# Perceiver cross-attention: attention values as TensorE's stationary operand, one output bank for a pair of groups

## The reference, cut to what matters

```python
xn, ln_lat = layer_norm(x, g1, b1), layer_norm(latents, g2, b2)   # context, latents; D = 256
q = ln_lat @ Wq                                                   # 16 heads of 64
k, v = split(concatenate([xn, ln_lat], axis=1) @ Wkv)
weight = einsum('bhld,bhnd->bhln', q, k) / 8, masked
weight = softmax(weight, axis=-1)
out = einsum('bhln,bhnd->bhld', weight, v) @ Wout
```

## Time and profile before

| | us |
|---|---|
| median of 3 runs (1054.81 to 1055.64) | 1055.42 |
| the profiled execution | 1054.65 |
| its span, first to last instruction | 1052.8 |
| TensorE busy, of the span | 1014.3 |
| VectorE busy | 809.3 |
| ScalarE busy | 666.8 |
| GpSimd busy | 204.1 |

### The profile page before, as it was taken

One profiled execution on the slowest core, in us unless ns is written; L12 is line 12 of the kernel. 1 busy time (PEld: TensorE's weight loads), 2 busy tenths in 40 slices (PEclk: granted clock), 3 DMA queues, 4 the chain that ended last, 5 costly groups with the idle time before them and its releaser, 6 DMA issues. The chain is left out here.

```text
span 1052.8 us, 25657 instructions
## 1 busy us (share of the span) xinstructions
PE 1014.3 (96%) x8683; PEld 943.1 (90%) x8684; DVE 809.3 (77%) x3001; ACT 666.8 (63%) x1550; POOL 204.1 (19%) x265
## 2 busy tenths in 40 slices
PE   6999999999999999999999998988999999999997
PEld 6899999999999999999999998977888999889887
DVE  7887777685877786787787777579879889889753
ACT  4765565674665665566565566478776876767753
POOL 0111111110111111111111111342015203263213
PEclk9999999999999999999999999999999999999999
DMA  6000000000000000000000100520010000110000
GB/s 208 18 13 2 10 1 1 12 12 4 12 2 0 12 13 3 13 2 0 12 13 2 35 2 2 166 38 2 1 41 21 2 1 21 35 48 2 1 22 21
DMA packets 28803, 21.64 MB, mean 21 GB/s; under 512 B 12094, under 2 KB 26267, under 8 KB 28699
## 3 DMA queue, kind: packets, MB, share of 16 engines
q1 hardware_dynamic: 28529, 20.21, 6.5%
q10 hardware_dynamic: 170, 0.07, 0.0%
HBM read 19.17 MB, written 1.05 MB: 19 GB/s over the span
## 5 line engine op out<-in xcount | busy, mean ns | idle before, releaser
L303 PEld LDWEIGHTS pv_ps<-v,pt 128*128 128x128 f32 x1792 | 214.9, 192 | 9.3 <-issue 2.8
L303 PE MATMUL pv_ps<-v,pt 128*128 128x65 f32 x1792 | 215.2, 272 | 3.2 <-DVE o L818 1.8
L796 DVE CUSTOM_DVE_ANT_0 s_sb<-s_ps,pen,mstate 128x256 f32<-128x256 f32 (+1 forms) x512 | 199.9, 446 | 13.9 <-issue 11.0
L510 ACT ACTIVATE probs<-s_sb,mbias 128x256 f32<-128x256 f32 (+1 forms) x512 | 203.2, 470 | 0.0
L670 POOL TENSOR_TENSOR o<-o,alpha 128x260 f32<-128x260 f32 x128 | 85.7, 669 | 561.3 <-ACT alpha L504 561.3
L519 ACT ACTIVATE pt<-turn 128x512 f32<-128x512 f32 x128 | 76.2, 595 | 123.0 <-PE turn L290 109.1
L290 PE MATMUL turn<-ident,probs 128*128 128x128 f32 x896 | 123.8, 278 | 0.1
L290 PEld LDWEIGHTS turn<-ident,probs 128*128 128x128 f32 x896 | 98.8, 145 | 9.5 <-issue 0.3
L818 DVE TENSOR_TENSOR o<-o,pv_ps 128x260 f32<-128x260 f32 x128 | 53.9, 421 | 46.1 <-PE pv_ps L303 34.7
L279 PE MATMUL s_ps<-kh,qh 64*128 64x256 f32 (+1 forms) x512 | 78.9, 304 | 2.9 <-DVE x L840 1.6
L768 DVE TENSOR_TENSOR kl<-proj,kh 128x512 fp32r<-128x512 f32 (+1 forms) x63 | 41.3, 655 | 51.5 <-ACT kh L497 51.0
(11 more groups left out here) (432 smaller groups left out, 2730.7 us busy)
## 6 DMA issues: line engine op xcount, KB each, us to landing
raw<-in_ctx SPq DMA_DIRECT2D x24, 128.0 KB, 2.0
f_wqkv_raw<-in_L_ffn_wqkv SPq DMA_DIRECT2D x6, 512.0 KB, 5.3
f_w_raw<-in_L_ffn_w SPq DMA_DIRECT2D x8, 256.0 KB, 5.1
f_w_raw<-in_L_ffn_w SPq DMA_DIRECT2D x2, 640.0 KB
wkv_raw<-in_L_xattn_Wkv SPq DMA_DIRECT2D x1, 1024.0 KB, 8.5
wout_raw<-in_L_xattn_Wout SPq DMA_DIRECT2D x1, 1024.0 KB, 12.5
f_wo_raw<-in_L_ffn_wo SPq DMA_DIRECT2D x2, 512.0 KB, 4.7
x<-in_x SPq DMA_DIRECT2D x1, 768.0 KB, 9.6
```

The lines of the kernel that those rows point to most:

```text
L303: last = pe.matmul(t.pv_ps[:, u, :], t.pt[g % 2][:, u, kt, :], t.v[:, kt, h, :], start=(kt == 0), stop=(kt == kts - 1))
L510: last = act.activation(t.probs[g % 2][:, u, 0:kts * P], t.s_sb[g % 2][:, u, 0:kts * P], ACT.Exp, bias=t.mbias[:, at:at + 1], scale=0.125)
L796: last = dve.tensor_tensor_reduce(out=t.s_sb[g % 2][:, u, 0:width], in0=t.s_ps[g % 2][:, u, 0:width], in1=t.pen[:, 0:width], scale=1.0, sc ...
```

## The change

Values become the stationary operand and the turned probabilities the moving one. A group then takes 4 matmuls (2 in a half body) with 64 stationary columns and 256 moving columns each, in fp32 as before; the first head's output goes to partitions 0 to 63 of `pv_ps`, the second's to 64 to 127. The bank now holds two groups, the even one in its first half and the odd one in its second. Since the output is the wrong way round, ScalarE copies the bank to a new buffer `ov` (`store_outputs`), TensorE turns it back with 4 transposes into the same bank (`turn_back`), and VectorE adds both groups at once (`add_outputs`). The 65th column goes: ScalarE's exponentials also give their sums (`accum_out`), and GpSimd adds these to `o`'s 65th column. TensorE's `weighted_values` of an odd group stands ahead of the projection in an even step, that of an even group behind the projection in an odd step, as before. `turn_back` opens an odd step. VectorE's addition comes in odd steps, behind `maxima`. Two small buffers and two semaphores of the opening are shared with others, to make room.

```diff
@@ -187,6 +187,10 @@
         if j < 0:
             return None if prev is None else (m - 1, j + NG, KINDS[prev])
         return None
+
+    def pair_at(m, kind, prev, j):
+
+        return at_step(m, kind, prev, j - 4) if j % 2 else None
 
     with nc.Block() as block:
         @block.sync
@@ -295,14 +299,21 @@
                 pe.wait_ge(s["pt_ready"], 16 * m + 2 * g + 2)
                 if g % 4 == 0:
                     pe.wait_ge(s["v_ready"], 4 * m + g // 2 + 2)
-                if g or not isinstance(m, int):
+                if g % 2 == 0 and (g or not isinstance(m, int)):
                     pe.wait_ge(s["o_added"], 8 * m + g)
-                for u in range(GU):
-                    h = 2 * g + u // QT
-                    for kt in range(kts):
-                        last = pe.matmul(t.pv_ps[:, u, :], t.pt[g % 2][:, u, kt, :], t.v[:, kt, h, :],
+                for kt in range(kts):
+                    for o, rows in enumerate((slice(0, DH), slice(DH, P))):
+                        last = pe.matmul(t.pv_ps[rows, g % 2, :], t.v[:, kt, 2 * g + o, :], t.pt[g % 2][:, QT * o:QT * o + QT, kt, :],
                                          start=(kt == 0), stop=(kt == kts - 1))
                 last.then_inc(s["pv_done"], 1)
+
+            def turn_back(m, g, kts):
+
+                pe.wait_ge(s["ov_stored"], 8 * m + g + 1)
+                for k in range(2):
+                    for qt in range(QT):
+                        last = pe.transpose(t.pv_ps[:, qt, k * P:(k + 1) * P], t.ov[:, k, qt * P:(qt + 1) * P], t.ident[:])
+                last.then_inc(s["o_turned_back"], 2)
 
             def turn_output(b, u):
 
@@ -384,9 +395,15 @@
                             scores(m, g, KINDS[kind])
                     if prev is None and j == 2:
                         pe.wait_ge(s["q_ready"], 4)
+                    pair = pair_at(m, kind, prev, j)
+                    if pair:
+                        turn_back(*pair)
                     now = at_step(m, kind, prev, j - 2)
                     if now:
                         turn_probs(*now)
+                    now = at_step(m, kind, prev, j - 3)
+                    if now and j % 2 == 0:
+                        weighted_values(*now)
                     if finish and j in (1, 2, 4, 5):
                         u = {1: 0, 2: 1, 4: 2, 5: 3}[j]
                         if u % 2 == 0:
@@ -437,7 +454,7 @@
                     now = at_step(m, kind, prev, j - 3)
                     if prev is None and j == 3:
                         pe.wait_ge(s["plan_rows"], 1)
-                    if now:
+                    if now and j % 2:
                         weighted_values(*now)
                     if kind and j == 3 and not final:
                         pe.wait_ge(s["v_ready"], 4 * m + (3 if KINDS[kind] == 2 else 4))
@@ -508,8 +525,15 @@
                 for u in range(GU):
                     at = GU * g + u
                     last = act.activation(t.probs[g % 2][:, u, 0:kts * P], t.s_sb[g % 2][:, u, 0:kts * P], ACT.Exp,
-                                          bias=t.mbias[:, at:at + 1], scale=0.125)
+                                          bias=t.mbias[:, at:at + 1], scale=0.125, accum_out=t.sums[:, at:at + 1])
                 last.then_inc(s["p_ready"], 1)
+
+            def store_outputs(m, g, kts):
+
+                act.wait_ge(s["pv_done"], 8 * m + g + 1)
+                if g >= 2 or not isinstance(m, int):
+                    act.wait_ge(s["o_turned_back"], 8 * m + g - 1)
+                act.activation(t.ov[:], t.pv_ps[:], ACT.Copy).then_inc(s["ov_stored"], 2)
 
             def store_turned(m, g, kts):
                 act.wait_ge(s["t_done"], 8 * m + g + 1)
@@ -542,6 +566,9 @@
                     now = at_step(m, kind, prev, j - 2)
                     if now:
                         store_turned(*now)
+                    now = at_step(m, kind, prev, j - 3)
+                    if now and j % 2 == 0:
+                        store_outputs(*now)
                     if finish and j in (1, 2, 4, 5):
                         store_output(b, {1: 0, 2: 1, 4: 2, 5: 3}[j], kind)
                     if final and j == 2:
@@ -669,6 +696,9 @@
                         pool.wait_ge(s["o_added"], 8 * m + g - 7)
                     pool.tensor_tensor(t.o[:, cols, :], t.o[:, cols, :],
                                        t.alpha[:, cols].unsqueeze(2).broadcast_to([P, GU, DH + 1]), ALU.mult).then_inc(s["rescaled"], 1)
+                    pool.wait_ge(s["rescaled"], 16 * m + 2 * g + 1)
+                    pool.wait_ge(s["p_ready"], 8 * m + g + 1)
+                    pool.tensor_tensor(t.o[:, cols, DH], t.o[:, cols, DH], t.sums[:, cols], ALU.add).then_inc(s["rescaled"], 1)
 
             pool.memset(t.o[:], 0.0).then_inc(s["state_zero"], 1)
             walk(pool, body)
@@ -811,15 +840,17 @@
                     dve.wait_ge(s["pv_done"], 8 * m + g - 1)
                 dve.tensor_copy(t.pt[g % 2][:, 2:4, :, :].rearrange("p u k q -> p (u k q)"), t.turn[1][:]).then_inc(s["pt_ready"], 1)
 
-            def add_output(m, g, kts):
-                cols = slice(GU * g, GU * (g + 1))
-                dve.wait_ge(s["pv_done"], 8 * m + g + 1)
-                dve.wait_ge(s["rescaled"], 8 * m + g + 1)
-                dve.tensor_tensor(t.o[:, cols, :], t.o[:, cols, :], t.pv_ps[:], ALU.add).then_inc(s["o_added"], 1)
+            def add_outputs(m, g, kts):
+                cols = slice(GU * (g - 1), GU * (g + 1))
+                dve.wait_ge(s["o_turned_back"], 8 * m + g + 1)
+                dve.wait_ge(s["rescaled"], 16 * m + 2 * g + 1)
+                added = t.o[:, cols, 0:DH].rearrange("p (h q) d -> p h q d", q=QT)
+                dve.tensor_tensor(added, added, t.pv_ps[:].rearrange("p q (h d) -> p h q d", d=DH), ALU.add).then_inc(s["o_added"], 2)
 
             def normalise_output(m, b, half):
                 cols = slice(half * H, (half + 1) * H)
                 dve.wait_ge(s["o_added"], 8 * m - 4 + 4 * half)
+                dve.wait_ge(s["rescaled"], 16 * m - 8 + 8 * half)
                 dve.reciprocal(t.inv[:, cols], t.o[:, cols, DH]).then_inc(s["inverse"], 1)
                 dve.wait_ge(s["inverse"], 2 * b - 2 + half + 1)
                 dve.tensor_tensor(t.onorm[:, :, half * 512:(half + 1) * 512].rearrange("p q (h d) -> p h q d", h=NG),
@@ -849,18 +880,20 @@
                 if kind == "latents":
                     dve.wait_ge(s["state_set"], b + 1)
                 for j in range(NG if kind else 6):
-                    now = at_step(m, kind, prev, j - 4)
-                    if now:
-                        add_output(*now)
-                    if finish and j in (0, 3):
-                        normalise_output(m, b, j // 3)
+                    if finish and j == 0:
+                        normalise_output(m, b, 0)
                     if kind and j == 4 and not final:
                         gained(m + 1, which)
                     if kind:
                         maxima(m, j, KINDS[kind])
+                    pair = pair_at(m, kind, prev, j)
+                    if pair:
+                        add_outputs(*pair)
                     now = at_step(m, kind, prev, j - 2)
                     if now:
                         store_turned(*now)
+                    if finish and j == 3:
+                        normalise_output(m, b, 1)
                     if finish and j in (1, 2, 4, 5):
                         output_lo(b, {1: 0, 2: 1, 4: 2, 5: 3}[j], kind)
                     if kind is None and j == 1:
@@ -2560,19 +2593,22 @@
...
-            t.v = sb("v", [P, KT, H, DH + 1])
+            t.v = sb("v", [P, KT, H, DH])
+            t.ov = sb("ov", [P, 2, L])
-            t.pv_ps = ctx.enter_context(nc.psum_tensor("pv_ps", [P, GU, DH + 1], F32))
+            t.pv_ps = ctx.enter_context(nc.psum_tensor("pv_ps", [P, 2, L], F32))
```

More of the change, by code:

```diff
@@ L159, in value_part @@
     def value_part(u):
-        return t.v[:, u % 2, (u // 2) * NG:(u // 2 + 1) * NG, 0:DH]
+        return t.v[:, u % 2, (u // 2) * NG:(u // 2 + 1) * NG, :]
     def load_norm(eng, which):
@@ L465, in _ @@
             project_keys(0, KB)
-            pe.wait_ge(s["keys_spread"], 1)
-            pe.matmul(t.pv_ps[0:B, 1, 0:NCH + 1], t.row_of[:], t.listed[:], start=True, stop=True).then_inc(s["keys_listed"], 1)
+            pe.wait_ge(s["flags_ready"], 3)
+            pe.matmul(t.pv_ps[0:B, 1, 0:NCH + 1], t.row_of[:], t.listed[:], start=True, stop=True).then_inc(s["flags_ranked"], 1)
             pe.wait_ge(s["w_lo"], 3)
@@ L502, in softmax_part @@
                 if not isinstance(m, int):
-                    act.wait_ge(s["rescaled"], 8 * m + g - 7)
+                    act.wait_ge(s["rescaled"], 16 * m + 2 * g - 14)
                 act.activation(t.alpha[:, GU * g:GU * (g + 1)], t.mdiff[:, GU * g:GU * (g + 1)], ACT.Exp,
@@ L679, in _ @@
             dve.memset(t.tick[:], 0.0).then_inc(s["s_read"], 2)
```

(17 more changed lines are left out.)

4 lines of the change are left out of this document (2 added, 2 removed).

## The result

The changed kernel takes 1147.2 us (median of 4 runs, 1143.9 to 1150.9); the kernel before took 1055.1 beside it. The ratio is 1.088, 95% interval 1.084 to 1.091: 92 us slower. 1106 was forecast, from 1074 to 1178.

What follows compares the result with a forecast made beforehand. TensorE bounds the cross stage, but would wait for VectorE's addition: 1054.65 + 27 (pair) + 13.5 (half) + 3.5 (last half) + 2.4 (latents) + 3 (opening) + 1 (drain) = 1105, forecast 1106 us, range 1074 to 1178.

Steps and rivals of the forecast that it cites:

- the rival without any overlap: `weighted_values`: the two heads' matmuls do not overlap, W = 1.87 us, w = 1.01; 1173 us in all; chance 0.22.
- a wait for the addition: TensorE idles some 2.4, 1.5 and 1.5 us before `weighted_values` in steps 1, 5 and 7 of a pair body.
- VectorE's wait for `kh`: Sign in the changed profile: this wait grows from 0.6 to about 1.8 us.
- The chain: Odd-step `weighted_values` waits through projection, `kl`, statistics, maxima and addition; steps 0 and 1 take 11.7 us, now 9.8.
- The price W: Time of `weighted_values` in a full group: 1.22 us, from five slots of 0.215 plus 0.15 for switching tile shape.
- the full-overlap rival: `weighted_values`: the two heads overlap fully, W = 1.01 us, w = 0.58; 1083 us in all; chance 0.12.
- the fifth slot: In-order starts let head 1's high pass run only with head 0's low pass: 8 records take 5 slots, 1.07 us.
- The prediction's last sentence: A granted clock below full after the new idle would add to all of it; no size given.
- the finishing bodies: Latents bodies that finish a batch: +0.8 us each, three times, 2.4 in all.
- the drain: End of the stage: a longer path from the last values to the sum, +1 us.
- VectorE's 1.5 us of lateness in step 1: Finishing latents bodies: statistics make VectorE late by some 1.5 us in step 1, the only step where maxima start late.
- The faster rival: VectorE's addition is in time, so TensorE's own sum holds: 8 x -2.3 us in pair bodies; 1033 us; chance 0.09.

Runs made afterwards that it cites:

- the fillers: Changed kernel plus unread identity transposes on TensorE in step 1 of pair bodies and steps 1 and 5 of half bodies: 1117.25 us, ratio 1.059.
- the last kernel: Kernel with addition ahead of maxima and values and copy late (1044.85 us), early order restored from step 4 of half bodies and in the drain: 1038.81 us.

## Why the prediction was right

*The range, and luck.* 1147.2 us is 41 above the forecast, and outside the forecast's own range (1090 to 1125). It falls in the wide range because that made room up to 1178 for the rival without any overlap, and this rival did not come true. So the mechanism was right, and that the wide range held is luck: a term that was left out, the clock, came to less than the room kept for something else.

*The mechanism.* The forecast was a wait for the addition, behind the maxima of the odd step. The changed profile shows it where the prediction put it (2.34, 1.23 and 1.19 us in steps 1, 5 and 7 of a pair body; 2.4, 1.5 and 1.5 were named), and the kernel with the addition first takes it away and all of the loss with it. VectorE's wait for `kh` grew from 0.61 to 1.81 us, as forecast, and TensorE is busy 87% of the stage.

*The chain.* Each link came out: the projection at 3.65 us (2.45 + 1.22 = 3.67), `kl` 2.36 later (2.34), the statistics' end 1.6 later (1.57), maxima 2.2. Steps 4 and 5 take 10.67 us, 10.8 forecast. Without the clock's loss the pair body is 42.75 us, 43.1 forecast, and the half body 37.35, 37.7 forecast.

*The price W.* 1.22 was forecast, 1.19 measured, by two errors that cancel, which is luck again: four slots, not five (full overlap, which I had given 0.12 as a rival), each of 0.216 as priced; but 0.18 us ahead of the group and some 0.15 at its ends where the forecast had 0.15 in all. So the full-overlap rival (the prediction once calls it the second) fails on its price, 1.01, not on its mechanism. The Trainium skill's rule for the swap ("TensorEngine Tiling (Array Packing)", section Performance Considerations) agrees with the trace, four slots instead of eight; the switch takes back a quarter of it, 0.18 of 1.74 - 1.02. The Trainium skill's statement that matmuls keep program order ("TensorE: Matmul & The Clock Gate", Part 3), from which I drew the fifth slot, did not tell the slots here, in either order of the heads; which two records share a start the trace does not name.

*The step that was mis-sized: the clock.* The prediction's last sentence said that a lower granted clock would add, and put no number to it. It was some 30 of the 41 us between 1106 and 1147. The earlier trace rows could not price it, but the trace they are from could. TensorE waits 1.38 us there at 650.65, in the last steps of the stage, and behind that:

```profile
651.30:654.70 3.40, 3.40 (x19) 3.40 (x18) 1.36 (x3) 1.47 (x3) 0.00 (x0) 0.50 0.00 0
```

Eight forecast idles of 2.4 us and sixteen of 1.5 asked for a term. How large one is for a given wait the runs do not settle: 2.35 us cost some 1.5 in seven pair bodies and nothing in the first, and the half bodies lost 7.4, 4.4 and 1.5 us to the clock (against 37.35 with the fillers) behind the same two waits. What decides between them is open. With that the sum of the parts is: pair bodies +37 (27 forecast), half +26 (13.5), opening +3.6 (3).

*Also too small: the finishing bodies and the drain.* Finishing latents bodies +13.7 (2.4), last half body and drain +10.7 (4.5). Waits in the first of them, in the changed kernel's trace:

```profile
252.84 0.65 PE L306 MATMUL pv_ps<-pt,v 128*64 128x256 f32 x4 [2.24 <-DVE o L848]
264.15 1.08 PE L306 MATMUL pv_ps<-pt,v 128*64 128x256 f32 x8 [0.83 <-DVE o L848]
```

I took VectorE's 1.5 us of lateness in step 1, and none in step 3. Part of it is the clock again (0.72 in the mean from 254 to 260 us). The second such body has the same waits but a full clock, and lasts 51.5 us where the two others last 53.1: so some 3 of the 13.7 us are the clock. With the addition first such a body lasts 48.95 at full clock: some 8 are the addition's place, and the last 3 stay even then. For the drain the shares are not separated.

*Smaller slips.* ScalarE copies the bank 64 times, that is 16 bodies' worth and not 8 (38.3 us busy in the changed kernel); it changes no term of the sum.

*The faster rival* (the addition in time, 1033 us) is what the kernel with the addition first makes true, and it shows that rival's price was too low as well: 1053.7, since its sum lacks the switch and the short waits for `kl`. Getting to 1038.8 took the later place of `weighted_values` too.

## What to carry to other kernels

When a change frees the busiest engine, write down for each of its buffers who must clear it and what stands ahead of that on the clearing engine: here one call in the wrong place on VectorE cost 93 us, and a change that was to relieve TensorE only did so (16 us, ratio 0.985) once that call and the place of the matmuls were put right. Price an idle TensorE twice: the wait itself, and the matmuls behind it, which may run at half the clock; look for an idle stretch anywhere in the trace before to see what it costs. And of a cheaper form of matmul, count the switch into its tile shape.

## What the runs showed that was not expected

- In seven of eight pair bodies 2.3 us without matmuls were followed by a granted clock of 0.50 for about 3 us, and the wait cost 1.5 us more than it lasted; in the eighth, behind the same wait, the clock stayed full. The Trainium skill ("TensorE: Matmul & The Clock Gate", Part 1) names the two levels and that idle time brings the lower one; the trace agrees, though not each such wait brought it. 128 matmuls whose result nobody reads saved 14 us.
- Eight fp32 records in two column halves start two by two, in four slots: 1.02 us against 1.87 in one half, and regardless of the order in which the two heads are written.
- Going to `128*64` tiles costs 0.18 us behind transposes (1.03 for 0.85) and 0.09 behind a projection (155.21 - 153.61 = 1.60 in the last kernel, before 1.51), and nothing behind scores (157.40 - 155.80 = 1.60 with two groups in a row, as before).
